# A graph attention layer on one core: probabilities turned by DMA instead of TensorE, even steps, four projection banks, layer norm in column chunks

## The reference, cut to what matters

```python
def attn(q, k, v, mask):                       # per graph and head
    scores = q @ k.T * 64 ** -0.5
    w = softmax(where(mask > 0, scores, -inf))
    return w @ v
edges = ln(attn(pe @ Wq1 + b, pe @ Wk1 + b, pe @ Wv1 + b, adj.T) + pe) * g1 + s1      # pass 1
nodes = ln(attn(pe @ Wq2 + b, edges @ Wk2 + b, edges @ Wv2 + b, adj) + pe) * g2 + s2  # pass 2
out = ln(nodes + gelu(nodes @ W1 + b1) @ W2 + b2) * g3 + s3                           # feed-forward
result = ln(x + out)                           # pe is x; 512 -> 2048 -> 512
```

## Time and profile before

| | us |
|---|---|
| median of 3 runs | 3141.88 (3140.71 to 3142.14) |
| profiled execution, span from the first to the last instruction | 3138.1 |
| PE busy | 3028.9 |
| DVE, ACT, POOL busy | 1765.9, 1422.4, 1507.8 |

### The profile page before, as it was taken

One profiled execution on the slowest core, in us unless ns is written; L12 is line 12 of the kernel. 1 busy time (PEld: TensorE's weight loads), 2 busy tenths in 40 slices (PEclk: granted clock), 3 DMA queues, 4 the chain that ended last, 5 costly groups with the idle time before them and its releaser, 6 DMA issues.

```text
span 3138.1 us, 54583 instructions
## 1 busy us (share of the span) xinstructions
PE 3028.9 (97%) x18944; PEld 2511.9 (80%) x18944; DVE 1765.9 (56%) x4762; ACT 1422.4 (45%) x3754; POOL 1507.8 (48%) x1418
## 2 busy tenths in 40 slices
PE   8999999999899999999998999999999999999996
PEld 7888888888788888878887888888888888888885
DVE  6777777777787878777776233333232333332334
ACT  5656565656566666566665322222222222222221
POOL 3656564656466667676764233333323333332324
PEclk9999999999999999999999999999999999999998
DMA  4121212221223233333334311101111111001101
GB/s 155 59 74 60 71 61 71 64 75 59 81 92 115 98 114 99 112 101 111 100 108 134 99 54 54 43 18 53 53 47 53 53 53 53 27 33 53 54 34 60
DMA packets 167312, 228.50 MB, mean 73 GB/s; under 512 B 7168, under 2 KB 72832, under 8 KB 167168
## 3 DMA queue, kind: packets, MB, share of 16 engines
q1 hardware_dynamic: 167168, 226.86, 22.2%
HBM read 159.73 MB, written 67.11 MB: 72 GB/s over the span
## 4 chain that ended last, share of the span: by engine, by line
PE 84%; DVE 11%; issue 2%; ACT 2%; DMA 1%; SPq 0%; DVEq 0%; POOL 0%; POOLq 0%; ACTq 0%
PE proj L798 28%; PE proj L1278 22%; PE score L1292 11%; PE pt L1292 11%; PE score L847 4%; DVE normed L627 4%; PE att_out L874 3%; PE pt L856 2%; PE att_turn L782 2%; DVE att_pt_lo L691 1%; DVE att_probs L684 1%; DVE att_k_lo L668 1%; ACT att_q_hi L440 1%; ACT att_probs L446 1%; DVE att_k_lo L665 1%
## 5 line engine op out<-in xcount | busy, mean ns | idle before, releaser
L1222 DVE TENSOR_TENSOR hidden_lo<-hidden,hidden_hi 128x512 fp32r<-128x512 f32 x256 | 215.1, 840 | 954.6 <-ACT hidden_hi L1063 954.6
L1070 ACT ACTIVATE hidden<-proj,ffn_bias 128x512 f32<-128x512 f32 x256 | 176.2, 688 | 1021.4 <-PE proj L1278 1021.4
L446 ACT ACTIVATE att_probs<-att_probs,att_minus_max 128x128 f32<-128x128 f32 x1024 | 397.0, 390 | 198.9 <-DVE att_minus_max L684 198.9
L85 POOL TENSOR_TENSOR pool_scratch<-pool_scratch 128x1 f32<-128x1 f32 x144 | 27.8, 193 | 856.1 <-DVE ffn_moments L1166 491.6
L684 DVE CUSTOM_DVE_ANT_0 att_probs<-score,att_mask 128x128 f32<-128x128 f32 x1024 | 226.5, 285 | 27.6 <-issue 19.3
L798 PE MATMUL proj<-source_hi,weight_k_hi 128*128 128x512 f32 x512 | 214.9, 420 | 20.7 <-DVE att_k_lo L668 20.7
L691 DVE TENSOR_TENSOR att_pt_lo<-pt,att_pt_hi 128x512 f16<-128x512 f32 x256 | 175.1, 684 | 94.2 <-ACT att_pt_hi L451 94.2
L798 PE MATMUL proj<-weight_v_hi,source_hi 128*128 128x512 f32 x512 | 210.2, 410 | 11.7 <-DVE weight_v_lo L640 11.2
L580 POOL TENSOR_TENSOR source_lo<-source_raw,source_hi 128x512 fp32r<-128x512 f32 x128 | 167.9, 1333 | 91.2 <-ACT source_hi L471 91.1
L1278 PE MATMUL proj<-source_hi,w_lo 128*128 128x512 f32 x512 | 203.5, 397 | 0.0
L1278 PE MATMUL proj<-source_lo,w_hi 128*128 128x512 f32 x512 | 202.9, 396 | 0.0
(11 more groups left out here) (155 smaller groups left out, 9098.1 us busy)
## 6 DMA issues: line engine op xcount, KB each, us to landing
att_tokens<-in_x SPq DMA_DIRECT2D x32, 1024.0 KB, 5.5
source_raw<-in_x_t SPq DMA_DIRECT2D x16, 1024.0 KB, 5.8
edges_t<-turned SPq DMA_DIRECT2D x64, 256.0 KB, 2.3
source_raw<-edges_t SPq DMA_DIRECT2D x16, 1024.0 KB, 7.8
att_query_raw<-in_x_t SPq DMA_DIRECT2D x16, 1024.0 KB, 7.9
nodes_t<-turned SPq DMA_DIRECT2D x64, 256.0 KB, 2.3
nodes<-normed SPq DMA_DIRECT2D x16, 1024.0 KB, 5.7
source_raw<-nodes_t SPq DMA_DIRECT2D x16, 1024.0 KB, 7.6
```

The lines of the kernel that those rows point to most:

```text
L446: nc.scalar.activation(probs[:, j, :], probs[:, j, :], ACT.Exp, bias=minus_max[:, j:j + 1], scale=-1.0, accum_out=row_sum[:, u % 2, j:j + ...
L1070: nc.scalar.activation(hidden[:, c % 2, :], up_bank[c % 2][:], ACT.Gelu, bias=bias_1[:, c:c + 1]).then_inc(activated, 1)
L1222: nc.vector.tensor_tensor(hidden_lo[:, c % 2, :], hidden[:, c % 2, :], hidden_hi[:, c % 2, :].bitcast(F32), ALU.subtract).then_inc(hidden_ ...
```

## The change

1. Probabilities are split first: after the exponentials ScalarE casts them to fp16 (`probabilities_high`, tile `p_hi`), VectorE takes the rest (`probabilities_low`, `p_lo`), each two instructions a step. SP then turns each tile, 128 x 1024 fp16, by one `dma_start_transpose` (`turn_probabilities`). `transposes`, `transposed_high`, `transposed_low` and the `pt_bank`s go.
2. `weigh` comes two steps after its scores, in one piece. Every step has the same form on TensorE: keys, queries, weigh, one value projection, scores; two of a group's value projections are made in the group before. Mask, maximum, exponentials and the split of a step are put in the next step of VectorE and ScalarE.
3. The two freed banks become projection banks 2 and 3.
4. The layer norm's sum and statistics are taken by steps of 128 columns in `add_weighed`, with four statistics a graph that are aggregated at the end. Centring moves to ScalarE, as a multiplication by `rstd` and an `offset` that GpSimd works out. The sums of odd and even groups lie in two tiles (`total`).
5. Loads and stores of SP are given out in another order, the source two groups ahead, tokens by 128 columns. The weights of pass 2 are split at the end of group 15 (values in step 2), the first pass's before its first group.

```diff
+PROJ_BANKS = 4
+    def load_source(sp, g, own):
+        sp.wait_ge(source_ready, C * g)
...
+        sp.dma_start(source_raw[:], source_view[n][:, :, bass.ds((g - n * NG) * GT, GT)]).then_inc(source_in, 16)
+    def turn_probabilities(sp, n):
+        wait(sp, weighed, n)
+        sp.sem_inc(sp_steps, 1)
+        sp.wait_ge(p_hi_ready, 2 * n + 2)
+        sp.sem_inc(sp_steps, 1)
+        sp.dma_start_transpose(pt_hi[:], p_hi[:].rearrange("p j i -> p (j i)")).then_inc(hi_turned, 16)
+        sp.wait_ge(p_lo_ready, 2 * n + 2)
+        sp.sem_inc(sp_steps, 1)
+        sp.dma_start_transpose(pt_lo[:], p_lo[:].rearrange("p j i -> p (j i)")).then_inc(lo_turned, 16)
 # SP, body(g), steady part
+            load_tokens(sp, g, own, 1)
+            if not below(g, 2):
+                store_turned(sp, g - 2, own, GB - 1)
...
+                sp.wait_ge(mask_ready, g + 1)
                 sp.dma_start(adj[:], passes[after]["adjacency"][:, bass.ds(following * GB, GB), :]).then_inc(adj_in, 16)
+            if own == 1 and after == 1:
+                sp.wait_ge(query_ready, C * (g + 1 - NG))
+                sp.dma_start(query_raw[:], query_view[:, :, bass.ds((g + 1 - NG) * GT, GT)]).then_inc(query_in, 16)
+            if not starts(g):
+                turn_probabilities(sp, C * g - 1)
+            load_tokens(sp, g, own, 2)
+            turn_probabilities(sp, C * g)
+            load_tokens(sp, g, own, 3)
+            load_source(sp, g + 2, own)
+            turn_probabilities(sp, C * g + 1)
...
+                load_tokens(sp, g + 1, after, 0)
+                store_turned(sp, g - 1, before, 0)
+            turn_probabilities(sp, C * g + 2)
+            if not starts(g):
+                store_turned(sp, g - 1, before, 1)
+                store_turned(sp, g - 1, before, 2)
                 if before == 1:
+                    store_tokens(sp, g - 1, 1 - parity)
 # ScalarE, a step (n = C * g + u - 1)
+                exponentials(n, (u - 1) % 2, 0)
                 key_high(g, own, u)
+                if u == 2 and not starts(g):
+                    centre(act, g - 1, 1 - parity, 0)
+                if u == 3 and not starts(g):
                     copy_turned(act, g - 1, 0)
+                exponentials(n, (u - 1) % 2, 1)
+                if u == 2 and not starts(g):
+                    centre(act, g - 1, 1 - parity, 1)
                 query_high(g, own, u)
+                if u == 3 and not starts(g):
                     copy_turned(act, g - 1, 1)
+                probabilities_high(n, 0)
+                probabilities_high(n, 1)
+                if u < 2:
+                    split_source(g, parity, range(2 * u, 2 * u + 2))
...
+                    value_high(g, parity, u + 2)
 # VectorE, a step
+                mask_and_maximum(n, g if u == 1 else None)
                 key_low(g, own, u)
                 query_low(g, own, u)
+                probabilities_low(n, 0)
+                probabilities_low(n, 1)
+                if u < 2:
+                    add_weighed(dve, g - 1, 1 - parity, before, u + 2)
+                    value_rest(g, parity, u + 2)
+                else:
+                    add_weighed(dve, g, parity, own, u - 2)
+                    value_rest(g + 1, 1 - parity, u - 2)
 # GpSimd, a group
+            value_low(g, parity, 1)
+            split_source(g, parity, range(0, 2))
+            add_bias(g, 1)
+            value_low(g, parity, 2)
+            split_source(g, parity, range(2, 4))
+            add_bias(g, 2)
+            value_low(g, parity, 3)
+            inverse_spread(pool, g - 1)
+            gain_and_shift(pool, g - 1, 1 - parity)
+            add_bias(g, 3)
+            split_queries(g + 1)
+            value_low(g + 1, 1 - parity, 0)
+            add_bias(g + 1, 0)
 # TensorE, a step
+                keys(g, parity, own, u)
+                if turning:
+                    turn(pe, g - 1, 1 - parity, 0)
                 queries(g, parity, own, u)
+                if u >= 2:
+                    weigh(pe, g, parity, u - 2)
+                elif not starts(g):
+                    weigh(pe, g - 1, 1 - parity, u + 2)
...
+                    values(g, parity, own, u + 2)
...
+                scores(g, u, 0)
+                scores(g, u, 1)
 # inside
+def probabilities_high(n, h):
+    if h == 0:
+        wait(act, hi_turned, 16 * n)
+    act.wait_ge(exped, UNIT * n + 4 * h + 4)
+    nc.scalar.copy(p_hi[:, 4 * h:4 * h + 4, :], probs[:, 4 * h:4 * h + 4, :]).then_inc(p_hi_ready, 1)
+def weigh(pe, g, parity, u):
+    n = C * g + u
+    wait(pe, attended_ready, n)
+    pe.wait_ge(hi_turned, 16 * (n + 1))
+    pe.wait_ge(lo_turned, 16 * (n + 1))
```

More of the change, by code:

```diff
@@ L222, in opens, with below, at @@
         return isinstance(group, int) and group % NG == 0 and group < last_group
+    def below(group, count):
+        return isinstance(group, int) and group < count
+    def at(group, value):
+        return isinstance(group, int) and group == value
     def over_passes(engine, body):
@@ L312, in value_bias_in @@
[L312 to L317, removed]
         sp.dma_start(source_raw[:], source_view[0][:, :, 0:GT]).then_inc(source_in, 16)
-        weight_in(0, "v")
+        weight_in(sp, 0, "v")
+        weight_in(sp, 0, "k")
+        weight_in(sp, 0, "q")
@@ new lines, in body @@
+            if after == 2:
+                sp.wait_ge(query_ready, C * NG)
+                for n in range(2):
+                    feed_forward.load(sp, n)
+            if isinstance(g, int) and g == NG + 1:
+                sp.wait_ge(shifted, GB * NG)
+                norm_rows_in(sp, 1)
+            if not starts(g):
+                turn_probabilities(sp, C * g - 1)
+            load_tokens(sp, g, own, 2)
+            turn_probabilities(sp, C * g)
+            load_tokens(sp, g, own, 3)
+            load_source(sp, g + 2, own)
@@ L400, in copy_turned @@
+            if not starts(g):
+                store_turned(sp, g - 1, before, 1)
+                store_turned(sp, g - 1, before, 2)
+                if before == 1:
+                    store_tokens(sp, g - 1, 1 - parity)
+            if after == 2:
+                for n in range(2, 4):
+                    feed_forward.load(sp, n)
+        over_passes(sp, body)
     def copy_turned(act, g, b):
@@ L507, in body @@
[L507 to L514 removed]
+            for u in range(C):
+                n = C * g + u - 1
+                first = starts(g) and u == 0
+                if u == 2 and own != after:
+                    act.wait_ge(projected, value_place(g, 3) + 1)
+                    if after == 1:
+                        weights_high(1, "v")
+                    else:
+                        feed_forward.high(act, 0)
+                        feed_forward.high(act, 1)
+                if u == 0 and starts(g):
+                    value_high(0, 0, 0)
+                    value_high(0, 0, 1)
+                if not first:
+                    exponentials(n, (u - 1) % 2, 0)
+                key_high(g, own, u)
+                if u == 2 and not starts(g):
+                    centre(act, g - 1, 1 - parity, 0)
+                if u == 3 and not starts(g):
@@ L522, in body @@
-                if u == 1:
-                    split_source(g, parity, range(0, 2))
-                if u == 2:
-                    split_source(g, parity, range(2, 4))
-                if turning:
-                    copy_turned(act, g - 1, 2)
-                if u == C - 1 and own == 1 and after == 1:
-                    split_queries(g + 1, range(C))
-                exponentials(g, u)
-                weights_ahead(g, own, after, u)
-                if turning:
+                if not first:
+                    probabilities_high(n, 0)
+                    probabilities_high(n, 1)
@@ L852, in transposes @@
[L852 to L876 removed]
+            if h == 0:
+                pe.wait_ge(proj_split, query_place(g, u) + 1)
@@ L935, in attention_passes, with feed_forward_pass @@
         "residual_biased": (biased, GB * last_group),
     }
-def feed_forward_pass(nc, ctx, m, block, weights, attention, source, nodes, x, b1, b2, gain, shift, out):
+def feed_forward_pass(nc, ctx, m, block, weights, attention, source, nodes, x, b2, gain, shift, out):
     def starts(group):
```

666 lines of the change are left out of this document (311 added, 355 removed).

## The result

The median of four runs is 3084.98 us (3084.09 to 3087.05), of before beside them 3141.3; the ratio is 0.9824, interval 0.981 to 0.9838. The kernel is 56 us faster. The forecast of 92 us had the direction right and was too large; the time lies in the 2985 to 3115 that it gave for its likeliest case.

A forecast was written before the change was run, and what follows sets the result against it. TensorE was taken to bound the old kernel, a ScalarE and VectorE ring the changed one. Groups of 47.9 and 49.9 us save 60.3 + 32.0 = 92.3 us, giving 3050 us; range 2945 to 3500.

The forecast's parts named there:

- its likeliest case: Whole kernel: the ScalarE and VectorE ring sets the period, transposes hidden; 3050 us, spanning 2985 to 3115, chance 0.45.
- So TensorE sets the pace: Kernel before, attention: TensorE is the bound, idle about 4%, with small holes of 2.59 and 2.82 us a group.
- the rival with TensorE as the bound: Changed kernel, attention: TensorE's floor of 45.56 us a group binds; 2943 up to 2985 us, chance 0.14.
- Part 2, the bare ring: Attention step through in-order ScalarE and VectorE: 10.47 to 11.16 us without once-a-group extras; the upper value was taken.
- Part 2, centrings ahead of the query: Two ScalarE centrings ahead of the query add 1.16 us a group, the wait for offsets 0.3.
- a rival (all rests contended): Attention: contended SBUF rests and adds lengthen the ring to 13.2 us a step, time about 3280 us; chance 0.12.
- Part 3, "I price them at nothing": SP's in-order waits ahead of a step's transposes cost nothing, up to 1 us a group if late.
- Part 3, T: Time for one transposing DMA in attention to land: 4.5 us, hidden while under 5.1.
- Both rivals with a transpose as the bound: Transposes set the attention step: engine throughput, T 5.6 to 8 us (chance 0.14); or serial blocks, time near 4390 us.
- Part 3, 2 us a group for the bulk loads of pass 2: Pass 2: the query load on SP's queue delays a group's first transposes, 0 to 6 us, taken as 2.
- Part 1 to 3, the clock: Attention: a granted clock falling from 1.00 was listed as a sign that the forecast is wrong, without a size.
- Part 4: Seams: moved weight and query splits, reordered first loads, last weighings in the feed-forward; 0, plus or minus 10 us.

The follow-up runs named there:

- experiment 5: Kernel before with three of each four TensorE probability transposes left out; 3139.6 us, ratio 0.9988.
- experiment 11: Kernel before with three of four VectorE centrings cut to 8 columns; 3092.14 us, ratio 0.9844.
- experiment 8: Changed kernel with a turned-tile store given out earlier, ScalarE's first two centrings behind the fp16 copies, and attention groups written out without loops; 2982.73 us, ratio 0.9493.
- Experiment 10: Changed kernel with each value rest on VectorE done twice from the second group on; 3139.46 us, ratio 0.9995.
- Experiment 3: Changed kernel with ScalarE's first two centrings moved behind the fp16 copies of the same step; 3018.47 us, ratio 0.9612.
- experiment 2: Changed kernel with one store of a turned tile given out by SP ahead of the transposes instead of behind them; 3060.99 us, ratio 0.9747.
- Experiment 12: Changed kernel with a third transposing DMA in each step, into a spare tile ahead of the real one; 3126.49 us, ratio 0.9955.
- Experiment 1: Changed kernel with each of the 256 transposing DMAs replaced by a plain DMA of the same tile; 3074.11 us, ratio 0.9789.
- experiment 9: Changed kernel with eight extra 128x128 TensorE transposes ahead of each key projection from the second group on; 3158.51 us, ratio 1.0048.
- experiment 6: Changed kernel with attention groups written out in a straight line instead of a loop of two groups; 3083.58 us, ratio 0.9817.
- experiment 7: Kernel before with attention groups written out in a straight line instead of a loop; 3141.0 us, ratio 0.9998.
- experiment 4: Changed kernel with both a turned-tile store given out earlier and ScalarE's first two centrings behind the fp16 copies; 3012.47 us, ratio 0.9594.

## Why the prediction came out as it did

The mechanism was right: the transposes leave TensorE, land in time, and the ring of ScalarE and VectorE sets the period. The forecast's sum was too large by 36 us.

- **"So TensorE sets the pace" was wrong.** It was read from 96% busy. Experiments 5 and 11 show that the old order gained 0 to 15 us from 84 us less TensorE work, and 48 us from 49 us less VectorE work. The sum did not fail by this, since its group length came from the ring. The time of the rival with TensorE as the bound, 2943 to 2985, was reached only by experiment 8, with three more edits.
- **Part 2, the bare ring, held, in part by luck:** 10.8 us, between 10.47 and 11.16. Inside it the way from the first maximum to the first rest took 6.41 us and not 5.95, and it ends in VectorE's `query_low` (519.54 to 520.21), which the list left out, and not in the fp16 copy. The two rests took 1.20 and the divide, add and statistics 2.60, each under its lower value. Taking the upper value gave 1.4 us a group too much (4 x 0.36). Experiment 10 confirms the ring. The aggregations: 0.66 us measured (11.46 - 10.8), 0.6 predicted.
- **Part 2, centrings ahead of the query, is the step mis-sized most:** 1.16 + 0.3 = 1.46 us predicted, 3.7 measured. The offset wait was 1.13 and not 0.3, a centring with two per-partition operands 0.8 and not 0.58, and the rests of the probabilities met GpSimd's gain and shift, for 1.2 us more. The last was named for a rival (all rests contended) but not given to the one step in which it happens. Experiment 3 took this excess out whole and gave back 66.5 us net.
- **Part 3, "I price them at nothing", failed for the stores of turned tiles.** I had compared the transposes with what stands ahead of them on SP, and not with what stands behind them. With the turned copies themselves the extra was 1.16 us predicted; measured, it is 3.0 us in one group (13.8 - 10.8) and 2.5 in the next, 2.8 on average. In the one the loop's end, for which I had no term, lies beside it. Experiments 2 and 12 show the path. But in the loops experiment 2 gave back only 0.7 us a group in pass 1 and 0.1 in pass 2 of the 1.6 by which this term was short; the rest stays with the copies and the loop's end and was not taken apart.
- **Part 3, T:** 3.2 us and not 4.5, as a piece costs less than the average packet. Experiment 12 added 135168 packets for 128 DMAs and raised the queue's share from 36.0% of 3085.3 to 41.5% of 3123.7 us: 23 us of engine time a DMA, 1.45 on each of 16 engines, 22 ns a packet instead of 66.7. Both rivals with a transpose as the bound fell with it.
- **Part 3, 2 us a group for the bulk loads of pass 2:** not there, 50.5 against 50.4.
- **Part 1 to 3, the clock:** named only as a sign of error, it came: 0.97 in attention, behind idle stretches of 2.4 us. I had no term for it. Its cost shows in TensorE's own time: the twelve score matmuls behind the idle at 494.48 took 2.72 us and not 1.43, and in the next group but one the twelve matmuls of the key projection (596.71) took 4.35 and not 2.77, 1.3 and 1.6 us more. As ScalarE and VectorE hardly wait for TensorE in after, little of this should reach the period; no run shows it apart.
- **Part 4:** the loops give 16 x (51.67 - 50.4) + 16 x (51.90 - 50.5) = 42.7 of the 52.8 us by which the span fell; the other 10 are seams and written-out groups, inside the plus or minus 10.

The account of a group by these terms: 47.9 - 1.4 (ring) + 0.1 (aggregations) + 2.2 (centrings) + 1.6 (turned copies, mean of both kinds of groups) = 50.4 us.

The Trainium skill, "VectorE: DVE Perf Modes", section "The three transpose paths", gives the DMA path 1309 ns a 128x128 block; this case's DMAs took 3.2 us for eight, 0.4 us a block, so the figure is not additive over the blocks of one DMA. Its "Advanced Engine Details and Errata", section "X-Bar Transpose (TRN2)", has transposing DMAs as fast as plain ones. Experiment 1's plain copies of the same tiles landed in 2.3 us against 3.1 to 3.2, so over a third longer here, and SP is held 1.25 us against 0.5.

Open: the parts of clock and of waits in experiment 5, what makes TensorE stop in the loop of pass 2 in experiments 5 and 9, and why pass 2 of experiment 8 stays 2 us a group above its floor.

## What to carry to other kernels

When every engine has idle time and short waits, take the bound from a ring of instructions, step by step, and write down for each in-order engine and queue what is behind a moved wait as well as what is ahead of it. Ask of each edit that gives a chain engine new work (here two centrings) whether it can stand behind the instruction that others wait for; that order was worth more than the whole change. Judge delays together: one that costs nothing alone (the loop's end) may be covered by another, and shows when that one is gone.

## What the runs showed of the hardware that was not expected

- A transposing DMA of 128 x 1024 fp16 within SBUF lands in 3.1 to 3.2 us, while SP is held 1.25 us by each; a plain one of the same tile lands in 2.3 us and holds SP 0.5.
- The end of a loop over groups leaves VectorE about 2.4 us without an instruction (ten times in after, 23.6 us in all, the longest 2.7; up to 2.9 in experiment 4). Its price was nothing in experiments 6 and 7 and 30 us between experiments 4 and 8.
- Less work for TensorE came with a lower granted clock (1.00 to 0.98 in experiment 5), and of 31.7 us left out only 10.7 left the busy time, with some 5 us of other work come in; and closing its idle time raised the clock from 0.98 to 1.00 in 78 to 700 us in experiment 8.
- Two VectorE subtractions of SBUF tiles took 1.30 us undisturbed and 2.52 beside GpSimd's gain and shift, whose own instructions then took 1.6 to 1.7 us instead of 1.3. A VectorE add of two SBUF tiles beside GpSimd's low part of the source took 0.76 us (522.43), hardly more than the 0.69 of the shortest such add in the earlier trace rows. So not every such pair costs.
- A VectorE centring cut from 512 to 8 columns still took 933 ns instead of 1432 beside GpSimd (experiment 11).
